# Up weights of a feed-forward layer kept by tiles of 128 columns instead of by rows

## The reference

```python
def _lora_linear(x, w, a, b):
    base = jnp.einsum('bsd,od->bso', x, w)
    low = jnp.einsum('bsr,or->bso', jnp.einsum('bsd,rd->bsr', x, a), b)
    return base + low * SCALING          # SCALING = 2, rank 16
h1 = _lora_linear(x, w1, lora_A1, lora_B1)   # 512 -> 1376
h3 = _lora_linear(x, w3, lora_A3, lora_B3)   # 512 -> 1376
g = jax.nn.silu(h1) * h3
return _lora_linear(g, w2, lora_A2, lora_B2) # 1376 -> 512
...
x = x + _L0_attn_ref(_L0_cond_ref(x, cond_128, ...), ...)
x = x + _L0_ffn_ref(_L0_cond2_ref(x, cond_128, ...), ...)
```

## Time and profile before

| | |
|---|---|
| median of 3 runs | 592.43 us (591.91 to 592.59) |
| the profiled execution | 592.94 us, span 590.7 us |
| PE | 578.0 us busy, 98% |
| PEld | 466.6 us, 79% |
| DVE, ACT, POOL | 236.5, 175.4, 184.5 us |
| granted clock of TensorE | 0.991 |
| line 1336 (up) in the chain that ended last | 41% |
| the same for line 1357 (down) | 20% |

### The profile page before, as it was taken

The page is one execution under the profiler, slowest core; times in us unless marked ns, Lnnn a source line. Parts: engine busy times, 40 slices in busy tenths (PEclk is TensorE's granted clock), DMA queues, the critical chain, the costliest instruction groups (busy, mean ns, idle before and its releaser), DMA issues.

```text
span 590.7 us, 8143 instructions
## 1 busy us (share of the span) xinstructions
PE 578.0 (98%) x3227; PEld 466.6 (79%) x3227; DVE 236.5 (40%) x340; ACT 175.4 (30%) x312; POOL 184.5 (31%) x148
## 2 busy tenths in 40 slices
PE   9999999799999999999999999999999999999997
PEld 6988988577787778887778888778888777888885
DVE  1434542799999851111641111244111234211112
ACT  3561224564655353332121111121111102211110
POOL 3438463699999585434200000000000000000000
PEclk9999999979999999999999999999999999999999
DMA  7975648445566773000019000007400001200001
GB/s 238 339 318 165 225 163 259 143 113 189 154 152 180 229 231 86 1 0 1 1 71 227 4 2 1 1 1 206 95 0 0 0 0 74 69 0 1 0 1 71
DMA packets 70735, 59.24 MB, mean 100 GB/s; under 512 B 45072, under 2 KB 61840, under 8 KB 69584
## 3 DMA queue, kind: packets, MB, share of 16 engines
q1 hardware_dynamic: 69840, 57.43, 32.1%
q10 hardware_dynamic: 864, 1.38, 0.6%
HBM read 40.94 MB, written 16.79 MB: 98 GB/s over the span
## 4 chain that ended last, share of the span: by engine, by line
PE 79%; SPq 7%; DMA 6%; POOL 4%; issue 1%; DVE 1%; ACT 1%; POOLq 0%; DVEq 0%
PE twin L1336 41%; PE twin L1357 20%; PE twin L1158 7%; SPq L463 4%; DMA x_dram<-rows 4%; PE twin L1178 3%; PE twin L1191 3%; PE twin L1233 2%; SPq L493 2%; DMA rows<-x_dram 1%; POOL probs L647 1%; POOL probs L655 1%; PE twin L1121 1%; DMA down_sb<-in_down_factors 1%; PE twin L1147 1%
## 5 line engine op out<-in xcount | busy, mean ns | idle before, releaser
L1049 DVE TENSOR_TENSOR gate<-twin,gate 128x512 f32<-128x512 f32 (+1 forms) x44 | 30.4, 691 | 244.5 <-PE twin L1336 244.5
L1336 PE MATMUL twin<-c_hi,f_lo 128*128 128x512 f32 (+1 forms) x352 | 96.6, 397 | 0.9 <-POOL f_lo L684 0.9
L1336 PE MATMUL twin<-c_hi,f_hi 128*128 128x512 f32 (+1 forms) x352 | 95.5, 393 | 0.0
L1336 PE MATMUL twin<-c_lo,f_hi 128*128 128x512 f32 (+1 forms) x352 | 95.4, 393 | 0.0
L1336 PEld LDWEIGHTS twin<-c_hi,f_lo 128*128 128x128 f32 (+1 forms) x352 | 65.7, 187 | 17.1 <-POOL f_lo L684 1.4
L1336 PEld LDWEIGHTS twin<-c_hi,f_hi 128*128 128x128 f32 (+1 forms) x352 | 65.5, 186 | 15.6 <-issue 0.3
L1336 PEld LDWEIGHTS twin<-c_lo,f_hi 128*128 128x128 f32 (+1 forms) x352 | 65.6, 186 | 15.5
L871 ACT ACTIVATE gate<-twin 128x512 f32<-128x512 f32 (+1 forms) x44 | 26.3, 598 | 170.4 <-PE twin L1336 170.4
L1357 PE MATMUL twin<-f_lo,gate_hi 128*128 128x512 f32 (+1 forms) x176 | 68.6, 390 | 0.0
L874 ACT CAST gate_hi<-gate 128x512 fp32r<-128x512 f32 (+1 forms) x44 | 27.3, 621 | 127.2 <-DVE gate L1049 127.2
L1357 PE MATMUL twin<-f_hi_head,gate_hi 128*128 128x512 f32 x128 | 50.2, 392 | 0.0
(11 more groups left out here) (150 smaller groups left out, 816.7 us busy)
## 6 DMA issues: line engine op xcount, KB each, us to landing
f_sb<-in_f SPq DMA_DIRECT2D x2, 2752.0 KB, 20.2
x_dram<-resid_stage SPq DMA_DIRECT2D x16, 256.0 KB, 2.1
rows<-x_dram SPq DMA_DIRECT2D x16, 256.0 KB, 3.5
q_t<-q_dram SPq DMA_DIRECT2D x8, 512.0 KB, 5.5
x_dram<-rows SPq DMA_DIRECT2D x16, 256.0 KB, 3.4
rows<-x_dram SPq DMA_DIRECT2D x8, 512.0 KB, 4.4
out<-rows SPq DMA_DIRECT2D x12, 256.0 KB, 2.0
x_sb<-in_x SPq DMA_DIRECT2D x2, 1024.0 KB, 7.9
```

The lines of the kernel that those rows point to most:

```text
L1049: dve.tensor_tensor(gate[0:w, h % 2, :], up_bank[2 * (h % 2) + 1][0:w, :], gate[0:w, h % 2, :], ALU.mult).then_inc(gate_ready, 1)
L1336: mm = pe.matmul(bank[0:w, :], f[:, c, :], c_part[:, c, :], start=(n == 0 and c == 0), stop=(n == 2 and c == DC - 1))
```

## The change

All three remaining parts of the up weights and the loaded weights themselves are kept by tiles: piece c of tile h stands at column (4h + c) x 128, in the last tile at 40 x 128 + c x 96. Each load is broken up to bring the data into that order: for each of the 4 row groups a transfer of 128 x 10 pieces of 512 bytes, and one of 128 x 4 pieces of 384 bytes for the last tile. A fold takes whole tiles: 512 columns (tiles 0 to 3), 96 (tile 10), 512 (tiles 4 to 7) and 256 (tiles 8 and 9), in that order. Splits and matmuls address the tiles. The number of matmuls stays the same.

```diff
-FOLD_N = HID // BLOCKS
+FOLD_TILES = ((0, 4), (10, 11), (4, 8), (8, 10))
...
-            f1_sb = sb("f1_sb", [P, DC, HID], room)
+            f1_sb = sb("f1_sb", [P, DC * HID], room)
...
+        def up_tile(w, h):
+
+            return w[:, h * DC * P:h * DC * P + DC * HW[h]].rearrange("p (c k) -> p c k", c=DC)
...
-            return ((f3_sb[:, :, cols], f3_hi[:, h, :, 0:w], f3_lo[:, :, cols]),
-                    (f1_sb[:, :, cols], f1_hi[:, :, cols], f1_lo[:, :, cols]),
+            return ((up_tile(f3_sb, h), f3_hi[:, h, :, 0:w], up_tile(f3_lo, h)),
+                    (up_tile(f1_sb, h), up_tile(f1_hi, h), up_tile(f1_lo, h)),
...
+        def fold_columns(n):
+
+            first, end = FOLD_TILES[n // len(up_folds)]
+            return slice(first * P, (end - 1) * P + HW[end - 1])
...
+            def load_up(to, w):
+
+                whole, last = HID // P, HW[-1]
+                to_whole = to[:, 0:whole * DC * P].rearrange("p (h c k) -> p c h k", c=DC, k=P)
+                for c in range(DC):
+                    sp.dma_start(to_whole[:, c, :, :], w[:, c, 0:whole * P].rearrange("p (h k) -> p h k", k=P))\
+                        .then_inc(ffn_loaded, 16)
+                sp.dma_start(up_tile(to, whole), w[:, :, whole * P:HID]).then_inc(ffn_loaded, 16)
...
-            sp.dma_start(f3_sb[:, :, :], f3).then_inc(ffn_loaded, 16)
-            sp.dma_start(f1_sb[:, :, :], f1).then_inc(ffn_loaded, 16)
+            load_up(f3_sb, f3)
+            load_up(f1_sb, f1)
...
-                        fold_at = n // len(up_folds) * FOLD_N
-                        dst = f[:, c, fold_at:fold_at + FOLD_N]
+                        first, end = FOLD_TILES[n // len(up_folds)]
+                        own = fold_columns(n)
+                        made = fold_bank[n % 4][:, 0:own.stop - own.start]
+                        if HW[first] == P:
+                            dst = f[:, first * DC * P:end * DC * P].rearrange("p (h c k) -> p c h k", c=DC, k=P)[:, c]
+                            made = made.rearrange("p (h k) -> p h k", k=P)
+                        else:
+                            dst = up_tile(f, first)[:, c, :]
...
-                    pe.wait_ge(ffn_loaded, 16 * 2)
+                    pe.wait_ge(ffn_loaded, 16 * 2 * (DC + 1))
...
-                fold_at = m // len(up_folds) * FOLD_N
-                pe.matmul(fold_bank[m % 4][:, 0:FOLD_N], a_up_s[:, factor, c * P:(c + 1) * P],
-                          b_up_s[:, fold_at:fold_at + FOLD_N], start=True, stop=True).then_inc(up_fold_filled, 1)
+                own = fold_columns(m)
+                pe.matmul(fold_bank[m % 4][:, 0:own.stop - own.start], a_up_s[:, factor, c * P:(c + 1) * P],
+                          b_up_s[:, own], start=True, stop=True).then_inc(up_fold_filled, 1)
...
-                        (1, ((f1_hi[:, :, cols], c_hi), (f1_hi[:, :, cols], c_lo), (f1_lo[:, :, cols], c_hi)),
+                        (1, ((up_tile(f1_hi, h), c_hi), (up_tile(f1_hi, h), c_lo), (up_tile(f1_lo, h), c_hi)),
...
-                        (0, ((f3_hi[:, h, :, 0:w], c_hi), (f3_hi[:, h, :, 0:w], c_lo), (f3_lo[:, :, cols], c_hi)),
+                        (0, ((f3_hi[:, h, :, 0:w], c_hi), (f3_hi[:, h, :, 0:w], c_lo), (up_tile(f3_lo, h), c_hi)),
```

More of the change, by code:

```diff
@@ L282, in adaln_attention_ffn @@
         with ExitStack() as room:
-            f1_sb = sb("f1_sb", [P, DC, HID], room)
+            f1_sb = sb("f1_sb", [P, DC * HID], room)
             up_sb = sb("up_sb", [STACK, 2 * D + HID], room)
         with ExitStack() as room:
-            f1_lo = sb("f1_lo", [P, DC, HID], room, F32R)
+            f1_lo = sb("f1_lo", [P, DC * HID], room, F32R)
             sb("room6_factors", [P, 2 * D], room)
@@ L297, in adaln_attention_ffn @@
         with ExitStack() as room:
-            f3_sb = sb("f3_sb", [P, DC, HID], room)
+            f3_sb = sb("f3_sb", [P, DC * HID], room)
         with ExitStack() as room:
-            f3_lo = sb("f3_lo", [P, DC, HID], room, F32R)
+            f3_lo = sb("f3_lo", [P, DC * HID], room, F32R)
         sb("room7", [P, DC * HID])
@@ L311, in adaln_attention_ffn @@
         with ExitStack() as room:
-            f1_hi = sb("f1_hi", [P, DC, HID], room, F32R)
+            f1_hi = sb("f1_hi", [P, DC * HID], room, F32R)
         sb("room8", [P, DC * HID])
@@ L356, in split_parts @@
         def split_parts(h):
-            w, cols = HW[h], slice(h * P, h * P + HW[h])
-            return ((f3_sb[:, :, cols], f3_hi[:, h, :, 0:w], f3_lo[:, :, cols]),
-                    (f1_sb[:, :, cols], f1_hi[:, :, cols], f1_lo[:, :, cols]),
+            w = HW[h]
+            return ((up_tile(f3_sb, h), f3_hi[:, h, :, 0:w], up_tile(f3_lo, h)),
+                    (up_tile(f1_sb, h), up_tile(f1_hi, h), up_tile(f1_lo, h)),
                     (f2_sb[0:w, h, :], f2_hi(h), f2_lo[0:w, h, :]))
         up_folds = [(f3_sb, c, 1) for c in range(DC)] + [(f1_sb, c, 0) for c in range(DC)]
+        def fold_columns(n):
+            first, end = FOLD_TILES[n // len(up_folds)]
+            return slice(first * P, (end - 1) * P + HW[end - 1])
         down_folds = (range(0, 6), range(6, 8), range(8, HC))
@@ L945, in _ @@
                         f, c, _ = up_folds[n % len(up_folds)]
-                        fold_at = n // len(up_folds) * FOLD_N
-                        dst = f[:, c, fold_at:fold_at + FOLD_N]
+                        first, end = FOLD_TILES[n // len(up_folds)]
[6 more added lines that the diff above has]
+                            dst = up_tile(f, first)[:, c, :]
                         dve.wait_ge(up_fold_filled, n + 1)
-                        dve.scalar_tensor_tensor(out=dst, in0=fold_bank[n % 4][:, 0:FOLD_N], scalar=LORA_SCALE,
+                        dve.scalar_tensor_tensor(out=dst, in0=made, scalar=LORA_SCALE,
                                                  in1=dst, op0=ALU.mult, op1=ALU.add).then_inc(up_folded, 1)
```

## The result

The changed kernel takes 589.49 us (median of 5 runs, 589.10 to 590.16), the kernel before 592.43 beside it (591.22 to 592.66): a ratio of 0.995, 95% interval 0.9933 to 0.9966, so 2.0 to 4.0 us less. The forecast was 588.8 us and faster by 3.6. The profiled execution took 589.84 us with a span of 587.6. Of all the executions in this document one, of the run with f1_hi alone by tiles, took 1,146.84 us at a granted clock of 1.0, nearly twice the nine others; no trace of it was kept, and the median given for that run counts it.

A forecast was written before the change was run, and what follows sets the result against it. PE was taken as the bound, busy for 578.0 of 590.7 us. The up matmuls' -4.1 us and the folds' +0.5, all else nothing, gave -3.6: 588.8 us against the median of 592.43, range 587.6 to 591.1.

The forecast's parts named there:

- The up matmuls: Feed-forward, f1_hi, f1_lo and f3_lo groups: tiles bring them to f3_hi's price, 4.1 us less (3.6 to 4.5).
- The cause named for it: Up matmuls: weight row groups lying 5,504 bytes apart make a matmul take 0.233 us instead of 0.227.
- The last tile: Eleventh feed-forward chunk, 96 wide, packed 384 bytes apart: nothing counted, 0 to 0.04 us a chunk.
- The folds: PE's folds by whole tiles, 512, 96 and 256 columns instead of 344: +0.5 us, between 0 and 1.1.
- DVE's folds: VectorE's additions of fold results: at most 2.7 us a group, hidden in 3.65 us between groups, price nothing.
- The loads: Ten f1 and f3 loads in small pieces: 17.3 us, landing at 44.6 us, before the first fold, price nothing.
- the line through the earlier trace: Loads: interpolation between 256-byte pieces (16.5 ns) and 1,024-byte pieces (41.9 ns), giving 25.0 ns for 512 bytes.
- The rival of dear pieces: Loads: 512-byte pieces cost as much as 1,024-byte ones, first fold waits 8.9 us, 597.7 us; stall 0.14, slower 0.06.
- SP's cover: SP's queue: eight more load issues take 4 to 6 us of its idle time before 38.53 us, price nothing.
- The total: Whole kernel: 3.6 us less, 588.8 us against the median (-0.6%).
- The rival of no gain: Up matmuls: their price does not come from the layout, so only the folds' 0.5 us remains, 592.9 us; chance 0.07.

The follow-up runs named there:

- the longer rows: Kernel before with f1_sb, f1_hi, f1_lo, f3_sb and f3_lo in rows of 1,408 columns instead of 1,376, two loads and 344-column folds kept: 588.55 us, ratio 0.9928.
- the 256-byte run: Changed kernel with each of its eight large load transfers split in two, in pieces of 256 bytes instead of 512: median 590.57 us of ten runs, ratio 0.9976.
- the second: Changed kernel, unaltered, measured again against the kernel before, beside a kernel with rows of 1,408 columns: 588.84 us against 592.74, ratio 0.9936.

## Why the prediction was right, and where not

**The up matmuls** (-4.1 us, 3.6 to 4.5): -4.22 us by the feed-forward stretch, and 5.44 us a chunk as expected. The price held because it was read from f3_hi, which already had the layout that the change gives to the others.

**The cause named for it** was wrong. The prediction set f3_hi's tiles against the rows and took "the 5,504-byte stride" as what the dear tensors share. They share it, but what costs is that it puts every second piece off the multiples of 256 bytes., with strides of 1,024 and 2,048 bytes, fit that just as well, and the prediction had no row that told the two apart. The number came out right since the tiles mend both, and here was luck: the rooms of the three tensors happen to start at multiples of 256 bytes, which the prediction did not ask. With f1_hi's tiles 128 bytes further, 1.94 us of the gain were gone. A reader who took the cause from it would have retiled a tensor where a longer row does.

**The last tile** (0): right, 5.56 us before and after. A tile of 96 columns packed 384 bytes apart has every second piece off again. Aligned starts would gain little: with them its steps are 228 to 232 ns (f3_hi, and the tensors in the longer rows), packed 230 to 234, which makes 0.04 us a chunk.

**The folds** (+0.5 us, 0 to 1.1): +0.53, by luck: within it two errors cancel. Four folds of 96 columns take 0.38 us, 0.095 each, below the 0.119 that I took as a floor (from a row with plain fp32 operands, `mix`, where those of the folds are fp32r); the projection behind them takes 0.09 us more, which I did not foresee. The 256-column ones are at 0.120, as assumed (0.121).

**DVE's folds** (0, hidden). DVE's timeline after the first group and the first short one:

```profile
48.61 2.48 DVE L974 SCALAR_TENSOR_TENSOR f_sb<-twin,f_sb 128x512 f32<-128x512 f32 x4 [3.60 <-PE twin L1172]
...
55.75 0.75 DVE L974 SCALAR_TENSOR_TENSOR f_sb<-twin,f_sb 128x96 f32<-128x96 f32 x4 [1.00 <-PE twin L1172]
```

Four long additions take 2.48 us, inside the 3.67 between two groups of folds, and DVE waits for PE, not PE for DVE.

**The loads** (0; last landing at 44.6 us): 42.7 us, no wait. The price of a piece can be read in the microsecond from 36 to 37 us, in the view of the transfers:

```profile
DMA packets 688, 0.35 MB, mean 348 GB/s; under 512 B 9, under 2 KB 688, under 8 KB 688
```

16 / 688 us = 23.3 ns a piece for one engine, against the 25.0 of the line through the earlier trace rows. A stall needed 29.3. The rival of dear pieces is out, but pieces do cost: the unbroken rows brought 5.6 MB in 12.7 us, some 440 GB/s. The Trainium skill's page "DMA: Bandwidth & Descriptors", Specifications, puts the smallest transfer for full rate at 512 bytes. By these rows a piece of that size still runs at about four fifths of what the long rows had.

**SP's cover** was mis-sized. The prediction counted 4 to 6 us for eight more issues, from 0.5 to 0.7 us each. The ten issues hold SP for 23 us. The store of the queries left at 39.96 instead of 38.53 us and nobody waited for it, because SP had been idle until 38.53 anyway; the 256-byte run, with its last issue at 46.06, is past that point.

**The total.** -3.6 us forecast, -3.7 by the stretches, -2.9 (2.0 to 4.0) by the first comparison of medians and -3.9 (2.8 to 4.7) by the second. The spans of the two profiled executions differ by 3.1 us, since the stretches that the change does not touch are 0.5 us longer in the changed kernel. The rival of no gain is out: with equal columns, the step from one matmul to the next is 227 or 233 ns by the start of the piece. The Trainium skill's page "TensorE: Matmul & The Clock Gate", section "LDWEIGHTS (loading the stationary operand)", lets the number of columns alone set the time of a weight load. The profile's records of the weight loads in line 1336, and in line 1361 after, do not contradict it, with a median of 188 ns in rows and in tiles alike; but it does not tell the step. Whether the load or something behind it takes the extra time is not shown.

## What to carry to other kernels

In a kernel that PE bounds, as this one with its weight pieces of 128 columns, compare steps of matmuls with equal shapes from start to start; where they differ by a few ns, look at the addresses at which the weight pieces start, and pad the row pitch (here 1,376 to 1,408 columns) so that all start at multiples of 256 bytes before re-tiling anything. If a load must be broken into small pieces, count how long its issues hold the queue as well as when it lands, and compare that with the first use: in the one stall that was traced the price was 2.7 us of waiting and 1.7 us more behind it, at half clock.

## What the runs showed of the hardware

- A matmul of 128 weight columns and 512 streamed columns (fp32r) follows the last after 227 ns where its weights start at a multiple of 256 bytes in each partition, and after 233 to 234 where every second piece starts 128 bytes off; a single piece off costs its own step and the one ahead of it 6 to 8 ns each. Why, and what other offsets cost (64 or 32 bytes), was not tried, and the steps with all pieces off (228 to 241 ns) are not explained. Nor is it clear why a matmul with 96 weight columns takes 228 to 232 ns even from aligned starts.
- Transfers of many pieces hold the engine that issues them: in the changed kernel the eight issues of line 424 took 0.69 to 5.46 us each (640 KB, 1,280 pieces), where a transfer of contiguous rows took 0.47 to 0.69. A transfer's own pieces alone do not set how long: with the longer rows the issue of the small causal mask, right behind the two loads in pieces of 5,504 bytes, took 4.18 us. What else does was not tried. In pieces of 256 bytes the loads moved 240 GB/s from 30 to 40 us, 17.3 ns a piece.
- The attention stage, untouched by every kernel here, varied by 1.6 us from one trace to another. What makes it vary stays open.
